# Selective scan laid out with channels on partitions, one drive and one scan of VectorE for each unit in turn

## What is computed

```python
def step(h, inp):
    d_t, x_t, B_t, C_t = inp                       # (b,k,d), (b,k,d), (b,k,16), (b,k,16)
    dA = jnp.exp(d_t[..., None] * As)
    h = dA * h + (d_t * x_t)[..., None] * B_t[:, :, None, :]
    y = jnp.einsum('bkdn,bkn->bkd', h, C_t)
    return (h, y)
...
dts, Bs, Cs = jnp.split(x_dbl, [DT_RANK, DT_RANK + D_STATE], axis=2)
dts = jnp.einsum('bkrl,kdr->bkdl', dts, dt_w)
As = -jnp.exp(A_logs).reshape(K, d, D_STATE)
out_y = selective_scan(xs, dts, As, Bs, Cs, Ds.reshape(K, d), dt_b)
```

## Time and profile before

| | |
|---|---|
| median of three runs | 963.06 us (962.89 to 965.89) |
| time of the profiled execution | 966.98 us |
| its span, first to last instruction | 965.2 us |
| mean granted clock of PE, share of full | 0.788 |
| busy: PE / DVE / ACT / POOL | 705.2 / 689.1 / 357.3 / 398.1 us |
| time to the end of the first scan | 67.86 us |
| first to last scan's end | 515.6 us |
| last scan's end to the first block's result | 27.7 us |

### The profile page before, as it was taken

How to read it: one execution, slowest core, us unless ns; L and a number is a source line. 1 busy time by engine, 2 the same in 40 slices (tenths; PEclk the granted TensorE clock), 3 DMA queues, 4 the chain that set the end, 5 groups by cost and what they waited for, 6 DMA issues and landing times.

```text
span 965.2 us, 8057 instructions
## 1 busy us (share of the span) xinstructions
PE 705.2 (73%) x2720; PEld 374.2 (39%) x2720; DVE 689.1 (71%) x652; ACT 357.3 (37%) x408; POOL 398.1 (41%) x204
## 2 busy tenths in 40 slices
PE   4937767676677576677777675665746759999998
PEld 3513232232232232222322221223532548888886
DVE  5369979889889889898898696694579143343432
ACT  3746336244263353452632233441410223232321
POOL 3237857768668577577685470000004100000000
PEclk9958569577695786775855877887959658999999
DMA  6030300300302103003012000502062000000000
GB/s 182 1 87 1 85 2 1 87 0 0 87 0 49 38 0 87 0 0 87 1 30 57 1 0 1 239 0 94 1 249 100 0 1 1 1 0 0 0 0 22
DMA packets 13926, 38.39 MB, mean 40 GB/s; under 512 B 2372, under 2 KB 3494, under 8 KB 13166
## 3 DMA queue, kind: packets, MB, share of 16 engines
q1 hardware_dynamic: 13904, 38.12, 13.9%
HBM read 20.73 MB, written 0.61 MB: 22 GB/s over the span
## 4 chain that ended last, share of the span: by engine, by line
PE 38%; DVE 35%; issue 13%; DMA 5%; ACT 4%; SPq 2%; POOL 1%; DVEq 1%; ACTq 0%
DVE area L1020 15%; PE ps L1588 13%; PE ps L1309 5%; DVE area L1008 5%; DMA stack<-area 4%; PE ps L1326 3%; PE ps L1601 3%; DVE area L323 2%; SPq L496 2%; PE ps L1292 2%; PE ps L1340 1%; DVE small L395 1%; PE ps L1267 1%; DVE area L990 1%; DVE area L1001 1%
## 5 line engine op out<-in xcount | busy, mean ns | idle before, releaser
L564 POOL TENSOR_TENSOR area<-area 128x1024 f32<-128x1024 f32 x126 | 324.4, 2577 | 156.5 <-DVE area L1020 156.5
L1309 PE MATMUL ps<-stack,sel 128*128 128x512 f32 x512 | 250.9, 595 | 138.2 <-DVE area L1020 83.9
L1020 DVE TENSOR_TENSOR_SCAN area<-ps,area 128x1024 f32<-128x1024 f32 x128 | 291.5, 2278 | 0.0
L695 ACT ACTIVATE ps<-ps,par_now 128x1024 f32<-128x1024 f32 x128 | 139.1, 1087 | 295.5 <-PE ps L1309 295.5
L1309 PEld LDWEIGHTS ps<-stack,sel 128*128 128x128 f32 x512 | 109.4, 254 | 316.6 <-DVE area L1020 142.1
L1008 DVE TENSOR_TENSOR area<-ps,area 128x1024 f32<-128x1024 f32 x128 | 154.7, 1208 | 57.4 <-PE ps L1309 54.2
L1588 PE MATMUL ps<-stack 128*128 128x512 f32 (+3 forms) x768 | 127.8, 326 | 0.4 <-DVE stack L1233 0.4
L1588 PEld LDWEIGHTS ps<-stack 128*128 128x128 f32 x768 | 117.0, 192 | 11.9 <-issue 2.6
L1326 PE MATMUL ps<-area,cst 128*32 128x512 f32 x512 | 96.1, 847 | 5.9 <-DVE area L1061 5.9
L422 DVE COPY area<-ps 64x1024 f32<-64x1024 f32 x32 | 39.3, 1227 | 85.6 <-PE ps L1588 85.6
L420 ACT ACTIVATE area<-ps 64x1024 f32<-64x1024 f32 x32 | 32.6, 1017 | 107.4 <-PE ps L1588 107.4
(11 more groups left out here) (282 smaller groups left out, 692.6 us busy)
## 6 DMA issues: line engine op xcount, KB each, us to landing
stack<-area SPq DMA_DIRECT2D x48, 256.0 KB, 4.6
area<-phi_scaled SPq DMA_DIRECT2D x1, 4104.0 KB, 25.3
stack<-tok SPq DMA_DIRECT2D x16, 256.0 KB, 5.0
area<-in_m_phi_dram SPq DMA_DIRECT2D x4, 1024.0 KB, 8.1
area<-phi_scaled SPq DMA_DIRECT2D x1, 4096.0 KB, 13.5
area<-in_q_t_dram SPq DMA_DIRECT2D x1, 1024.0 KB, 13.6
area<-in_dft_dram SPq DMA_DIRECT2D x1, 784.0 KB
area<-in_m_u_dram SPq DMA_DIRECT2D x1, 768.0 KB, 6.4
```

Of the source, the lines that this page charges most:

```text
L564: pool.tensor_tensor(state[:, i % 8, :], state[:, i % 8, :], c_rep[:, b, :], MUL).then_inc(sig("weighed"), 1)
L695: act.activation(steps_pair(i), steps_pair(i), ACT.Exp, scale=par_now[:, i:i + 1]).then_inc(sig("decayed"), 1)
L1020: dve.tensor_tensor_scan(state[:, i % 8, :], steps_pair(i), drive[:, i % 4, :], 0.0, MUL, ADD).then_inc(sig("scanned"), 1)
L1309: mm = pe.matmul(ps[:, bank + h, :], sel[:, 4 * (j % 2) + v, :], stack[:, b, what, j // 2, h * HALF:(h + 1) * HALF], start=True, stop=True)
```

## The change

A unit is now one state of all 128 channels: partitions are channels throughout, and what differs from unit to unit is which of the 16 rows of B and C it uses. The two images' blocks come one after the other (`block_of`: image, then direction), no longer in turn, and all loops are written out.

- Delta and delta times x (`u_in`) stay where softplus leaves them, so `stack`'s DMAs, `sel`'s high/low halves and ACT's in-place exponentials are gone. ACT makes the decay from delta in SBUF (`make_decay`, four buffers) and copies the spread C row from PSUM (`copy_c`, four buffers).
- PE projects 16 rows of B and C (`project_rows`, 32 columns, 4 beside each other), and spreads one row of each over the partitions for every unit (`spread`: two matmuls with 32 rows for B into banks 0, 1 or 2, 3, two for C into banks 4, 5).
- The drive multiplies in place in PSUM (`drive_pair`), and stands directly ahead of its own scan.
- The sum over states and directions, and the removal of the mean over channels, become one accumulation in banks 6 and 7 over all 64 units of an image (`sum_state`: two plain f32 matmuls of 128 columns for each unit, reading the state in image order).
- POOL makes the three sums of softplus and `u_in` (`soft_sum`). DVE has one operation of 512 columns for each block beside drives and scans (`split_rows`).
- Banks 4 and 5 are shared in turn by C, the z projection, the B and C rows from block 1 on, the spectra and others (`turns`, `shared_free`): a job there waits until the previous one has been copied out.
- The spectra, the second image's convolution output, both gates, and the first image's layer norm and projection are done between units. The layer norm's weight and bias are folded into the projection.

```diff
--- before.py
+++ after.py
-            def slot(k, s):
-                n, b, i = split_slot(k, s)
-                nk, nb = following(k, b)
-                if i < GROUPS - 1:
-                    drive_unit(n, b, i + 1)
-                elif not ends(k, b):
-                    drive_unit(n + 1, nb, 0)
-                wait(dve, sig("decayed"), GROUPS * n + i + 1)
-                wait(dve, sig("driven"), GROUPS * n + i + 1)
-                wait(dve, sig("summed"), 4 * n + i // 4 - 1)
-                dve.tensor_tensor_scan(state[:, i % 8, :], steps_pair(i), drive[:, i % 4, :], 0.0,
                                        MUL, ADD).then_inc(sig("scanned"), 1)
...
+            def drive_unit(u):
+
+                n, b, k, i = block_of(u)
                 if i == 0:
+                    dve.wait_ge(sig("u_ready"), n + 1)
+                dve.wait_ge(sig("b_spread"), u + 1)
+                dve.tensor_tensor(drive_pair(u), drive_pair(u), u_in[:, n % 2, :], MUL).then_inc(sig("driven"), 1)
+
+            def scan_unit(u):
+
+                dve.wait_ge(sig("decayed"), u + 1)
+                dve.wait_ge(sig("driven"), u + 1)
+                wait(dve, sig("summed"), u - STATES + 1)
+                dve.tensor_tensor_scan(state[:, u % STATES, :], decay[:, u % DECAYS, :], drive_pair(u), 0.0,
...
+            for m in range(PAIRS):
+                n, p = divmod(m, 8)
+                for u in (2 * m, 2 * m + 1):
+                    drive_unit(u)
+                    scan_unit(u)
+                if p == ROWS_AT and n < BLOCKS - 1:
+                    split_rows(n + 1)
+                elif (n, p) == (2, 4):
+                    dve.wait_ge(sig("skip_done"), 1)
+                    dve.tensor_tensor(x_res[:], x_res[:], banks(4), ADD).then_inc(sig("skip_added"), 1)
...
+            def spread(u, what, bank):
+
+                n, b, k, i = block_of(u)
+                for h in range(2):
+                    at = 32 * (2 * what + h)
+                    mm = pe.matmul(ps[:, bank + h, :], sel[at:at + 32, i, :], bc_rows[at:at + 32, n % 2, :],
+                                   start=True, stop=True)
+                return mm
...
+            for m in range(PAIRS):
+                before, beside = sums_of(m)
+                pe.wait_ge(sig("scanned"), 2 * m + 1)
+                if 2 * m + 2 < UNITS:
+                    spread_b(2 * m + 2)
+                if m in JOBS:
+                    job(*JOBS[m])
...
+                for u in before:
+                    sum_state(u)
+                pe.wait_ge(sig("scanned"), 2 * m + 2)
+                if 2 * m + 3 < UNITS:
+                    spread_b(2 * m + 3)
+                if 2 * m + 2 < UNITS:
+                    spread_c(2 * m + 2)
+                for u in beside[:1]:
+                    sum_state(u)
+                if 2 * m + 3 < UNITS:
+                    spread_c(2 * m + 3)
+                for u in beside[1:]:
+                    sum_state(u)
+                if m == 0:
+                    gate(0)
+                    gate(1)
...
+            for m in range(PAIRS):
+                n, p = divmod(m, 8)
+                if (n, p) == (4, 0):
+                    first_image(0)
+                if 2 * m + 4 < UNITS:
+                    make_decay(2 * m + 4)
+                if p == Z_AT and n < BLOCKS - 1:
+                    soft(n + 1, "z")
+                elif p == ROWS_AT and n < BLOCKS - 1:
+                    rows_round(n + 1)
...
+                if 2 * m + 2 < UNITS:
+                    copy_c(2 * m + 2)
+                if 2 * m + 5 < UNITS:
+                    make_decay(2 * m + 5)
+                if 2 * m + 3 < UNITS - 1:
+                    copy_c(2 * m + 3)
+                if p == Z_AT and n < BLOCKS - 1:
+                    soft(n + 1, "exp")
+                    soft(n + 1, "one_plus")
+                elif p == ROWS_AT and n < BLOCKS - 1:
+                    soft(n + 1, "log")
+                    soft(n + 1, "rest")
```

More of the change, by code:

```diff
@@ L44 @@
 CONST = {}
-for _name, _n in (("ident", P), ("pair", P), ("red", 4 * 32), ("mean", P), ("center", P),
+for _name, _n in (("ident", P), ("pair", P), ("pick", NS), ("low", 1), ("mean", P), ("center", P),
                   ("heads", P), ("split", P), ("merge", 4 * P), ("rank", E), ("sign", 1)):
@@ L786, in _ @@
-            act.activation(size2[:].rearrange("p (r n) -> p r n", r=2), spec[:, 0:2, :],
-                           ACT.Square).then_inc(sig("size_sq"), 1)
-            def weigh_ident(u):
+            conv_out(0)
+            act.preload_act_table_set("natural_log_exp_and_others")
+            for step in ("z", "exp", "one_plus", "log", "rest"):
+                soft(0, step)
+            rows_round(0)
+            make_decay(0)
+            make_decay(1)
+            copy_c(0)
+            make_decay(2)
@@ new lines, in _ @@
+            for h in range(2):
+                act.wait_ge(sig("y_done"), h + 1)
+                act.activation(half(squares, h), ps[:, 6 + h, :], ACT.Square).then_inc(sig("y_squared"), 1)
+            for h in range(2):
+                act.wait_ge(sig("y_var"), h + 1)
+                own = half(rstd, h)[64:128]
+                link(act.activation(own, ps[64:128, 2 + h, :], ACT.Ln, bias=eps5[64:128]))
+                act.activation(own, own, ACT.Exp, scale=-0.5).then_inc(sig("y_rstd"), 1)
@@ L1420, in _ @@
[L1420 to L1423 removed]
+            pe.wait_ge(*after("sel_ready"))
+            spread_b(0)
+            spread_b(1)
+            spread_c(0)
+            convolution(1, 1)
+            spread_c(1)
+            pe.wait_ge(sig("consts_in"), 16)
@@ L1653, in constants @@
     part("ident")[:] = np.eye(P)
-    for v in range(4):
-        part("red")[:, v * 32:(v + 1) * 32] = (p[:, None] // NS + 8 * v) == np.arange(32)[None, :]
-    sel = np.stack([(p[:, None] % 64 - 8 * v) == p[None, :] // NS for v in range(8)], 1).astype(np.float32)
+    part("pick")[:] = p[:, None] % NS == np.arange(NS)[None, :]
+    part("low")[:, 0] = np.where(p % 32 < NS, 0, -1)
     part("pair")[:] = 0.5 * (p[:, None] // 2 == p[None, :] // 2)
```

843 lines of the change are left out of this document (401 added, 442 removed).

## The result

The changed kernel took 977.51 us (median of 4 runs, 975.08 to 978.43), the kernel before 964.01 on the same chip (4 runs, 962.89 to 965.89): ratio 1.0134, 95% interval 1.0108 to 1.0161. It is slower by 1.3%, where 878 us was forecast. Its profiled execution took 978.43 us with a span of 976.6.

A forecast was written before the change was run, and what follows sets the result against it. VectorE was taken to bound the scan, with 10% of holes. Front -23.2, scans -44.3 and tail -18.2 make -85.7: 966.98 becomes 881.3, adjusted to the runs' median and stated as 878 us; range 848 to 922.

The forecast's parts named there:

- the step that failed: TensorE in the scans: four spreads at 0.28 and four sum records at 0.43, 2.84 us a unit, hidden behind VectorE.
- The row split: VectorE's 512-column operation in seven blocks: +4.9 us for the work, +17.5 for waiting 2.5 each for rounded rows.
- VectorE's units: Each scan waits for the drive directly ahead: 0.14 us more a unit, 3.45 in all, +17.8 over 127 units.
- my rival by it: The scan's wait for its drive costs nothing, by the page's semaphore rule: 860 us, chance 10% within a rival of 18%.
- The drive in place in PSUM: VectorE's drive writing PSUM in place: taken as 0 extra, at most 5 us in all.
- What leaves VectorE: During the scans, softplus sums go to POOL, -45.6 us, and the waits of before go, -49.6.
- The front: Stretch up to the first scan's end: 44.7 us in place of 67.9, -23.2.
- The tail: Stretch after the last scan: some 9.5 us in place of 27.7, -18.2.
- The first block: Extra work between its units: units 2 and 4 come 1.4 us late each, the split 7.8 beyond its ordinary wait, +8.
- the sum into `x_res`: VectorE's sum, 1.2 us, together with the spectra's turns in bank 4, 1.5: +2.7 in the scans.
- my second rival: TensorE's clock stays below 0.68 in the scans, over 4.38 us a unit, so the kernel is slower; chance 5%.
- The row groups: Spread matmuls on different groups of 32 rows run beside each other: 2.45 us a unit instead of 3.0, not counted.

The follow-up runs named there:

- e1: The changed kernel with sums of states reading every state straight, without the return to image order: 906.23 us, ratio 0.9383 to the kernel before.
- e3: e1 plus the z and row projections reading `xc` as it lies, so no strided read on TensorE: 898.26 us, ratio 0.9306 to the kernel before.
- e5: On e4, ScalarE's exp and one_plus moved behind the rounding of the rows, log and rest to the next pair: 908.16 us, ratio 0.9371.
- e10: On e4, TensorE's first sum of states moved right behind the projection in the two pairs with one: 898.95 us, ratio 0.9297 to the kernel before.
- e4: On the changed kernel, GpSimd writes products in image order into its own ring and TensorE reads them straight: 904.58 us, ratio 0.9381 to the kernel before.
- e12: On e4, VectorE does two units' drives and then their two scans: 925.45 us, ratio 0.9587 to the kernel before.
- e7: On e4, drives go to an SBUF ring of two, a unit ahead of their scans; C copies have two buffers: 1091.98 us, ratio 1.1265.

## Why the prediction was wrong, point by point

The profiled execution of after is 97.1 us above my 881.3: 3.2 in the front, 91.8 in the scans (563.1 against 471.3), -0.1 in the tail, and 2.2 behind it, in code that both share, whose cause stays open.

**TensorE: the step that failed.** At full clock "a record of a plain f32 one 0.43", and with it 2.84 us a unit, was taken for every sum of states. It holds for the straight half of the blocks; the turned ones take 0.86, and their unit 4.04, above VectorE's 3.50. Between after and e1 the loop from the first scan's end to the last's shrinks from 563.1 to 489.2: 73.9 of the 91.8 are this one operand. Of them 42.7 are the drives' waits (44.4 less the 1.7 that e1 keeps) and 22.9 the split's, whose chain has these sums in it; the other 8 were not followed. I had argued at length about which of two clocks would be granted and took the two durations in the earlier trace rows for those two clocks; the clock came out as I said (0.93), and it decided nothing. The projections of `xc`, turned as well, make 3.7 more in the loop (489.2 in e1 to 485.5 in e3).

**The row split.** Forecast 2.5 a block by ScalarE's order "whatever TensorE's clock". Even with no turned operand on TensorE (e3) it waits 30.3, of which 9.2 in the first block and 3.5 in each other. The size is near, the reason was in part wrong: e5 took ScalarE's passes away and gained nothing, e10 moved TensorE's sums and cut the wait, and TensorE's clock does enter: in e4 the same sum took 3.78 us at 0.50 ahead of a wait of 6.60, and 1.98 at 1.00 ahead of one of 3.94. How the wait divides among the links in each block is not shown, nor what brought the clock down in the one block and not in the other.

**VectorE's units.** 3.45 forecast, 3.50 measured: 1.29 to 1.30 to the scan instead of 1.26. The term is +24 instead of +17.8, and e12 confirms that it comes from the dependence. The rule of the Trainium skill (VectorE: DVE Perf Modes, "The DRAIN you can't avoid"), no extra time for a semaphore after each operation, does not hold for a drive and the scan that needs it; my rival by it, 860, is out.

**The drive in place in PSUM** cost next to nothing, as taken (1218 against 1208 ns, scan 2287 against 2278). e7 shows that its place is worth far more than I asked: with the drive in SBUF a scan beside GpSimd takes 0.95 us longer.

**What leaves VectorE**, softplus sums and the old waits, left it. GpSimd's products are at 2363 ns, and its product group alone stands idle for 181 us; TensorE waits 2.5 us for them in all, so GpSimd hardly bounds anywhere.

**The front** came out at -20 instead of -23.2: the turned z projection takes 3.65 instead of 1.7, and `u_in` 2.07 instead of 1.23. The latter reads `xc` turned; whether that or ScalarE's decays beside it cost the 0.8 us was not tried.

**The tail** is right, 9.4 against 9.5. **The first block** cost 12.3 over its units and the split itself in e3, against 2.5 and 8 forecast; the sum into `x_res` cost 1.9 there (5.36 from drive to drive), against 2.7 with the spectra.

**The rivals.** The case that came true has the place of my second rival, TensorE as the bound and the kernel slower, with 5%, but not its mechanism. None of the rivals held a TensorE that is slow at full clock. The row groups of the Trainium skill (TensorE: Matmul & The Clock Gate, Part 3), which I left out of the sum, do run beside each other: four records take 0.43 us from start to start (112.69 to 113.12). At the 0.28 each of my sum a turned unit would have been 0.7 us longer still, as an estimate.

## What to carry to other kernels

Price a matmul by the access pattern of its moving operand, and look in the trace for a record with that pattern at a known clock; where duration and clock change together, check that nothing else changed. If one engine must read turned, let an engine with slack write turned instead: here GpSimd did it for nothing, and the same change went from 1.3% slower to 6 and 7% faster (e4, e10). Before an engine is packed tight, list what it contends with: in e7 one operand moved from PSUM to SBUF made each scan 0.95 us longer, and the kernel as a whole took 20% more than e4.

## What the runs showed of the hardware that was not expected

- A plain f32 matmul of 512 columns whose moving operand is read with 32 elements between neighbours takes 0.86 us a record, at full and at half clock alike (before at 546 and 540); read straight, 0.43 and about 0.86 (before at 548, e4 at 315.7). Other strides were not tried. The Trainium skill (SBUF — State Buffer, "Door 1: The DMA port swizzle") says that strides beyond 4 fp32 lose the full bandwidth of a 16-byte line; the direction agrees at full clock, a factor is not given there, and I had not weighed it. By the same rule GpSimd's scattered writes in e4 might have cost something, and they did not.
- A VectorE operation that waits for the one directly ahead of it costs 0.19 us a unit (3.50 in e4 against 3.31 in e12).
- Behind 1.84 us in which TensorE waited, the granted clock stood at 0.50 once (e4 at 315.7) and at 1.00 another time (e4 at 378.3); it had been at 1.00 ahead of both.
